# Turning V with block transposes on VectorE instead of TensorE, and two rotation sums on GpSimd

## What is computed

```python
q = (xn @ wq.T)...; k = (xn @ wk.T)...; v = (xn @ wv.T)...
q = q * cos + rotate_half(q) * sin
k = k * cos + rotate_half(k) * sin
probs = softmax(q @ k.T / sqrt(128) * key_scale + causal)
attn = probs @ v
x + (attn @ wo.T) * silu(ffn(xn))
```

## Time and profile before

| | |
|---|---|
| median of 3 runs | 1327.3 us |
| the profiled execution: time | 1326.8 us |
| the profiled execution: span of its instructions | 1324.6 us |
| TensorE busy | 1303.3 us, 98% |
| VectorE busy | 953.7 us, 72% |
| ScalarE busy | 972.5 us, 73% |
| GpSimd busy | 427.0 us, 32% |
| granted TensorE clock, mean | 0.999 |

### The profile page before, as it was taken

The page is one execution under the profiler, slowest core; times in us unless marked ns, Lnnn a source line. Parts: engine busy times, 40 slices in busy tenths (PEclk is TensorE's granted clock), DMA queues, the critical chain, the costliest instruction groups (busy, mean ns, idle before and its releaser), DMA issues.

```text
span 1324.6 us, 22633 instructions
## 1 busy us (share of the span) xinstructions
PE 1303.3 (98%) x7000; PEld 1106.3 (84%) x7000; DVE 953.7 (72%) x2438; ACT 972.5 (73%) x2529; POOL 427.0 (32%) x345
## 2 busy tenths in 40 slices
PE   8899999999999999999999999999999999999998
PEld 7688788888888888888888888888888888888876
DVE  7776678777777677777767777767777767777776
ACT  6877577877778777778777777777677877776874
POOL 5413312423214332233414124141431433224323
PEclk9999999999999999999999999999999999999999
DMA  6000000201101000000100001010000101002124
GB/s 230 24 1 21 25 8 9 65 28 53 40 17 32 15 25 8 16 16 16 27 5 24 8 16 32 0 32 0 24 24 0 32 8 32 8 20 95 52 82 150
DMA packets 23530, 43.66 MB, mean 33 GB/s; under 512 B 2496, under 2 KB 2752, under 8 KB 23488
## 3 DMA queue, kind: packets, MB, share of 16 engines
q1 hardware_dynamic: 20896, 38.74, 9.5%
q10 hardware_dynamic: 2592, 4.40, 0.9%
HBM read 34.74 MB, written 8.39 MB: 33 GB/s over the span
## 4 chain that ended last, share of the span: by engine, by line
PE 92%; ACT 3%; DVE 3%; issue 1%; DMA 0%; DVEq 0%; ACTq 0%
PE bank_b L510 19%; PE bank_a L510 18%; PE bank_b L604 13%; PE o_ps L604 12%; PE pv_ps L597 10%; PE pair L581 8%; PE pair L588 6%; PE pair L577 2%; PE pair L579 1%; PE o_ps L510 1%; PE bank_a L567 1%; ACT x_sb L1000 1%; ACT probs L918 0%; ACT probs L907 0%; ACT rot L857 0%
## 5 line engine op out<-in xcount | busy, mean ns | idle before, releaser
L399 POOL TENSOR_TENSOR rot<-rot,tab 128x512 f32<-128x512 f32 x160 | 207.1, 1296 | 593.2 <-ACT rot L858 592.9
L907 ACT ACTIVATE probs<-probs,row_min 128x128 f32<-128x128 f32 (+1 forms) x512 | 225.7, 447 | 0.2
L926 ACT ACTIVATE pT_hi<-pair 128x768 fp32r<-128x768 f32 x128 | 104.0, 812 | 164.5 <-PE pair L588 163.7
L918 ACT ACTIVATE probs<-probs,row_inv 128x128 f32<-128x128 f32 (+1 forms) x512 | 190.6, 445 | 22.5 <-DVE row_inv L1305 22.1
L1275 DVE TENSOR_TENSOR pT_lo<-pair,pT_hi 128x768 fp32r<-128x768 f32 x128 | 121.6, 950 | 86.1 <-ACT pT_hi L926 85.9
L382 POOL TENSOR_TENSOR w_hi<-raw,zero 128x512 fp32r<-128x512 f32 x74 | 85.0, 1148 | 243.4 <-PE bank_a L510 126.5
L510 PE MATMUL bank_a<-xT_hi,w_hi 128*128 (+1 forms) x376 | 149.9, 399 | 0.2 <-DVE xT_lo L1145 0.2
L510 PE MATMUL bank_b<-xT_hi,w_hi 128*128 (+1 forms) x376 | 149.8, 398 | 0.0
L510 PE MATMUL bank_b<-xT_hi,w_lo 128*128 (+1 forms) x376 | 146.8, 390 | 0.0
L510 PE MATMUL bank_a<-xT_hi,w_lo 128*128 (+1 forms) x376 | 146.8, 390 | 0.0
L510 PE MATMUL bank_a<-xT_lo,w_hi 128*128 (+1 forms) x376 | 146.3, 389 | 0.0
(11 more groups left out here) (181 smaller groups left out, 3277.3 us busy)
## 6 DMA issues: line engine op xcount, KB each, us to landing
raw<-w_seq SPq DMA_DIRECT2D x76, 256.0 KB, 2.6
gate_scratch<-b_raw ACTq DMA_DIRECT2D x16, 256.0 KB, 2.0
out<-y_sum SPq DMA_DIRECT2D x16, 256.0 KB, 2.0
x_sb<-x SPq DMA_DIRECT2D x3, 1024.0 KB, 11.2
mid<-x SPq DMA_DIRECT2D x7, 256.0 KB, 2.8
mid<-gate_scratch SPq DMA_DIRECT2D x7, 256.0 KB, 3.5
raw<-x SPq DMA_DIRECT2D x7, 256.0 KB, 2.7
raw<-gate_scratch SPq DMA_DIRECT2D x7, 256.0 KB, 2.9
```

The source lines that it names most:

```text
L399: nc.gpsimd.tensor_tensor(v, v, tab[:, s:s + SEQ].unsqueeze(1).to_broadcast([P, 2, SEQ]), ALU.mult).then_inc(sin_done[kind], 1)
L907: a = nc.scalar.activation(s, s, ACT.Exp, bias=row_min[:, j % 2, i:i + 1], scale=-1.0, accum_out=row_sum[:, i:i + 1])
L918: a = nc.scalar.activation(s, s, ACT.Copy, scale=row_inv[:, i:i + 1])
L926: nc.scalar.activation(pT_hi[:, :, :], pair[j % 2][:, :, 0:ROWS], ACT.Copy).then_inc(pThi_done, 1)
```

## The change

V is no longer turned on TensorE, except the V of unit 0 in the opening. `turn_v_blocks(count, half)` on VectorE reads V from `bank_a` and writes it turned into `v_T` in SBUF, by sixteen transposes a unit in two halves of eight. Each takes 32 partitions by 4 x 32 elements, so the source starts at partition 32j and the result at partition 32i, with j in the inner loop. The second half follows `rows_low` of item 2. `copy_vT` goes for all units but the first. K of unit u+2 waits for both halves (`vturn_done`). `v_high` and `v_low` read `v_T`. The additions of cosine and sine parts for K and H0, from the third unit's on, go from VectorE (`rotate`) to GpSimd (`add_halves`), directly behind the product with the sines. The lists of ScalarE, VectorE and GpSimd are put in another order in places, in the units and in the opening.

```diff
+            def add_halves(kind, count):
+                dst = k_full[:, :] if kind == K else cosx[:, BUF[kind], :]
+                pool.wait_ge(sin_done[kind], count)
+                pool.wait_ge(cos_done[kind], count)
+                nc.gpsimd.tensor_tensor(dst, cosx[:, BUF[kind], :], rot[:, BUF[kind], :], ALU.add)\
+                    .then_inc(sum_done[kind], 1)
...
                     if c3 is not None:
                         sin_product(K, c3)
+                        add_halves(K, c3)
                         sin_product(H0, c3)
+                        add_halves(H0, c3)
...
-                pe.wait_ge(vT_done, c2)
+                pe.wait_ge(vturn_done, value(pe, 2 * u + 2))
                 project(K, bank_a, WK, x_2, w_2)
...
-            if not last:
-                if ahead:
-                    bank_free(K, c3)
-                else:
-                    pe.wait_ge(vT_done, c2)
-                turn_v()
...
+        def v_high(turned, used):
             act = nc.scalar
+            act.wait_ge(vturn_done, value(act, 2 * turned))
+            act.wait_ge(pv_done, used)
+            nc.scalar.activation(v_hi[:, :, :], v_T[:, :].rearrange("p (k d) -> p k d", k=BLOCK_TILES),
                                  ACT.Copy).then_inc(vhi_done, 1)
...
+        def turn_v_blocks(count, half):
+            dve = nc.vector
+            dve.wait_ge(proj_done[V], count)
+            dve.wait_ge(v_ready, value(dve, count - 1))
+            src = bank_a[:, :].rearrange("p (t i a) -> p t i a", t=BLOCK_TILES, i=4)
+            dst = v_T[:, :].rearrange("p (t d) -> p t d", t=BLOCK_TILES)
+            for i in range(2 * half, 2 * half + 2):
+                for j in range(4):
+                    ins = nc.vector.transpose(dst[32 * i:32 * i + 32, :, 32 * j:32 * j + 32],
+                                              src[32 * j:32 * j + 32, :, i, :])
+            ins.then_inc(vturn_done, 1)
```

## The result

The kernel after takes 1360.3 us (1360.2 to 1360.8), the kernel before beside it 1327.4: ratio 1.025, 95% interval 1.024 to 1.026. The forecast was 1341. The direction was right; the loss is 33 us where 14 were forecast.

A forecast was written before the change was run, and what follows sets the result against it. TensorE bounds the kernel: 1326.8 us, +16.7 for block-transpose waits less the removed transposes, -1 side branch, -1 opening, summed there as 1340.5, forecast 1341 us. Range 1309 to 1361; the forecast case's own 1331 to 1361 (0.60).

The forecast's parts named there:

- what bounds the kernel, and where the waits come: TensorE, busy 98%, bounds it; per loop unit scores 0 wait 0.57 us for pT_lo, K 0.93 us for v_T.
- the removal: Taking V's four transposes off TensorE gains 0.48 us in each of 31 units, 14.9 us.
- the step d: Time from one block transpose to the next on VectorE: 0.32 us, each held by changed partitions (0.29 + 0.03).
- The flowing rival: Changed source does not hold VectorE: d = 0.21, no waits, 1311 us; chance 0.29 with or without GpSimd's delay.
- GpSimd's sums: Rival: v_low beside GpSimd's K sum takes 1.24 us, not 0.68, delaying rows_low: 9 us more; no separate chance.
- K's start behind its wait: In the loop K starts 0.05 us after VectorE's last block transpose ends, at 611.48 instead of 610.55.
- The other changes of place have no row that is late; nothing: Reordered list entries, apart from the opening's normalisations of blocks 2 and 3, cost 0 us.
- 1 us of gain for the opening: Normalisations of blocks 2 and 3 move forward into ScalarE's idle time: between -2.3 and +1, taken as -1 us.
- The side branch: Units 0 to 7: sometimes gives TensorE work between V and K, sometimes holds K more; 1 us taken off.
- The longer rival: A block transpose outlasts an elementwise instruction: 1361 us at d = 0.36, 1405 at 0.45; chance 0.06 above 0.36.

The follow-up runs named there:

- no_turn: Kernel before without TensorE's four transposes of V and nothing in their place, V used unturned: 1315.0 us, ratio 0.991.
- one_source: Kernel after with every block transpose reading partitions 0 to 31 of the bank instead of 32j to 32j+31: 1323.8 us, ratio 0.998.
- pe_written_out: Kernel after with TensorE's list written out for all units instead of a loop, other engines unchanged: 1357.4 us, ratio 1.023.
- lists_no_turn: Kernel after without the sixteen block transposes, V copied unturned by ScalarE, new lists and GpSimd's sums kept: 1321.4 us, ratio 0.996.
- rows_low_first: Kernel after with rows_low of item 0 and the first V's low part again ahead of item 1's row_inverse in the opening: 1362.3 us, ratio 1.026.
- result_changes: Kernel after with the block transposes' two loops exchanged, so the result moves at every step and the source at one in four: 1363.0 us, ratio 1.027.

## Why the prediction was right or wrong

First a slip in the record: 1326.8 + 16.7 - 1 - 1 is 1341.5, not 1340.5. It changes nothing below; the column of forecasts above goes by the terms.

**Right: what bounds the kernel, and where the waits come.** One wait ahead of scores 0 and one ahead of K, the same in each unit of the loop, by the releasers that were named.

**Right: the removal, in the loop.** 0.48 us, by `no_turn`, and in its units 0 to 7 as well. *Open at the end*: -1.4 was forecast for the last units and +1.3 measured in `no_turn`, but 2.2 us of that are its drawn-out `v_low`, which the kernel after doesn't have (0.68 us in all its units).

**Right: the step d.** 0.32 forecast, 0.325 measured, and `one_source` shows the reason to be the right one. The two parts of the number were off and made up for each other: an instruction takes 0.312 us and not 0.29, the gap behind it 0.014 and not 0.03. The Trainium skill gives 311 ns for 128x128 in bf16 in "VectorE: DVE Perf Modes", section "The three transpose paths"; the measured length agrees, for fp32 and 32 partitions. The flowing rival (1311) fell with it. *GpSimd's sums* fell too: `v_low` kept its 0.68 us in every unit, and putting the sums back changed nothing in the loop.

**The term that failed in the loop: K's start behind its wait.** I took 0.05 us from VectorE's end to TensorE's start, from an instruction with a fixed address. Measured are 0.33, of which `pe_written_out` takes 0.28 away. So the block transposes came to 1.33 us a unit in the mean (26.5 over twenty) instead of 1.03. The rest of that term held in sum: the first block transpose started 0.13 us behind V's last matmul instead of 0.21 in three units of four, which made up for the longer step. Over the loop the term fell short by 5.9 us.

**The term that failed outside: the lists.** "The other changes of place have no row that is late; nothing", and 1 us of gain for the opening. Measured, with the sums on GpSimd, are +6.1 us up to unit 8 and +2.4 in the loop. I looked at the rows of before at their old places and costed no order of the new opening lists; two entries, read against each other, would have shown `rows_low` of item 0 behind a wait for the exponents of item 1. Unit 0 starts between 44.2 and 45.6 us in the seven kernels with the old opening lists and between 46.7 and 48.7 in the ten with the new ones. Which entries make it later stays open; the normalisations do not.

**The side branch.** I took 1 us off. In unit 3 the routing work of the side branch stands ahead of the first half on VectorE, and scores 0 wait for both:

```profile
209.75 1.43 DVE L1235 TENSOR_TENSOR mid<-mid,gate 128x256 f32<-128x256 f32 x4
211.10 2.57 DVE L1277 STREAM_TRANSPOSE v_T<-bank_a 32x128 f32<-32x128 f32 x8
213.71 0.96 DVE L1299 TENSOR_TENSOR pT_lo<-pair,pT_hi 128x768 fp32r<-128x768 f32 x1
```

```profile
214.72 0.38 PE L590 MATMUL pair<-k_parts,q_hi 128*128 128x256 f32 x1 [2.68 <-DVE pT_lo L1299]
```

The same scores waited 0.67 us before; that unit is 4.3 us longer, while units 4 to 7 are 0.1 longer each. The block transposes up to unit 8 came to 7.8 us against the 7.2 of the sum (8 x 1.03 - 1). That agrees, but up to there single executions differ by as much as 3.6 us without an edit that explains it, so it confirms little.

**The longer rival** gave 1361 for d = 0.36. The time is that of the rival, but d is not: that the time of 1360.3 us lies just inside the range is luck.

## What to carry to other kernels

Work moved to an engine that is busy for 72% costs what it delays, not what it lasts: read, at the exact place in the list, what stands behind it and who waits; over the twenty units of the loop the same sixteen instructions cost 26.5 us in one place and 7.3 (9.6 less 2.3) in another. Price a new wait with all that stands behind it in the waiting queue, computed addresses and the slower restart (here 0.28 and 0.11 us) included. And when a change reorders lists, cost each exchange on its own, the opening above all: here the lists and the sums on GpSimd cost 7 us without the thing that they were made for.

## What the runs showed of the hardware

A block transpose of 32 partitions by 128 fp32 elements out of PSUM takes 0.312 us with steps of 0.325 when source or result moves to other partitions, and 0.263 us with steps of 0.197 when neither does.

The granted clock is a cost of waits that the sum did not have. In the opening its mean over 15 us fell from 0.89 to 0.66 (0.66 in `lists_no_turn` as well, so by the lists and not by the block transposes), in the tables by stretch of before and of after:

```profile
45.00:60.00 15.00, 11.76 (x64) 9.84 (x63) 11.29 (x33) 13.96 (x36) 6.97 (x7) 0.89 0.07 19
```

```profile
45.00:60.00 15.00, 9.62 (x45) 8.26 (x45) 8.05 (x22) 11.97 (x29) 9.66 (x8) 0.66 0.19 52
```

In unit 3 the same idle time led to 1.2 GHz in some executions and not in others, worth 2.4 us. It can widen the spread, too: 5.6 us over five runs of `rows_low_first`, 2.3 us over the 21 runs of before beside `result_changes` (but 0.6 over four of after).

VectorE's subtraction with both inputs in SBUF went from 0.68 to 1.77 us beside GpSimd's splitting of weights, and to 1.78 beside its addition. With one input in PSUM the same subtraction kept its 0.68 us beside that addition. Nor is it always VectorE that is held: in the kernel after, K's sum on GpSimd starts while `v_low` runs; `v_low` keeps 0.68 us, and the sum takes 1.60 where H0's takes 1.29.
